# Global attention: VectorE evicts the first transposed group of each unit, GpSimd makes the mask rows of every second head

## The chip, the cores and the metric

The kernel runs on one NeuronCore of a Trainium2 chip. The metric is the device time of one execution in microseconds (us), lower is better. In the text PE is TensorE, DVE is VectorE, ACT is ScalarE, POOL is GpSimd.

## The reference

The input `x` has 2048 rows of 128 values. Three residual stages follow each other: half a feed-forward/local-attention stack of six layers, one global attention, and the same stack again.

```
x = x + 0.5 * ffn_stack(layernorm(x))     # six layers, local attention in windows of 32
x = x + global_attention(layernorm(x))    # the stage that the change touches
x = x + 0.5 * ffn_stack(layernorm(x))
```

The global attention, cut to what matters (L = 2048 rows, 4 heads of 32 values, `x` already normalised):

```
q_in = x @ Wq.T
q, k, v = split(q_in @ Wqkv.T + bqkv)                  # 4 heads each
scores = einsum(q, k) / sqrt(L)
thr[l, h] = sigmoid(relu(q_in) @ Wop.T @ W2.T + b2) * L + WINDOWS[h]
dist[l, m] = m - l   (1e18 where m < l)
s2 = where(dist > thr, -1e18, scores) + scores
out = softmax(s2) @ v
```

Keys in front of the query are masked, so a tile of 128 queries needs only the keys from its own first row on.

## The kernel before

The queries are cut into 16 tiles `t` of 128 rows. Tile `t` needs `m = 16 - t` blocks of 128 keys. A **unit** `n = 2t + pair` is one tile with two of the four heads (`e = 0, 1`), so there are 32 units (`G_UNITS`), and the number of keys falls from 2048 in units 0 and 1 to 128 in units 30 and 31. A unit's keys are cut into **chunks** of up to 512 columns, `c = 0, 1, ...` (four for m = 13 to 16, three for 9 to 12, two for 5 to 8, one for 1 to 4). All four engines run a fixed, hand-written order over the units, and semaphores join them:

- DVE makes the mask rows of a unit ahead of time (`mask_rows`, L743: compare the distance with a threshold per query and multiply by -1e18, SBUF to SBUF, a whole row of keys at once). For each chunk and head it adds mask and scores from PSUM and takes the maximum (`masked_scores`, L756), then reduces the maxima (L764) and signals `g_nmx`. In even units from 4 on, behind chunk 0, it does `update` (L726, L730) for the tile that was attended before: it adds the result to the residual. Some updates also hold layer-norm statistics (L489, L493) or a layer-norm (L502) for the next stage.
- ACT takes the exponential of a whole row for both heads (L974), and evicts the transposed probabilities from PSUM to SBUF, group by group (L964, signal `g_pt_sb`). It does the groups of unit n-1 first and then the exponentials of unit n. It also copies the attended output (L958).
- PE computes scores (L1294), transposes the probabilities in **groups** of up to four 128x128 blocks (`transpose_group`, L1302), multiplies with the values (`attend`, L1313) and transposes the output (L1332). The groups of a unit are those of head e = 0 in order of chunks, then those of e = 1. They use three PSUM banks in turn (`t_bank`: two of ps_t and one of ps_h), so group g waits until group g-3 has been evicted.
- POOL does two small operations for each layer-norm part (`layer_norm_rstd`, L412 and L414), and otherwise waits until the stage is over.

PE's order in iteration n of its loop: the scores of chunks 0 and 1 of unit n; then, for odd n, `attend((n-3)/2)`, or for even n the small output transpose; then the groups of unit n-1 two at a time, with a later chunk of unit n behind each two. An **odd iteration** thus has an attend and an **even iteration** has none.

The rows of the profile name tiles by memory: `arena` is the big SBUF block that holds scores, masks and probabilities; `w_vo` and `w_qk` hold the masks of odd units. The score chunks lie in `ps_a` and `ps_s`.

Of the kernel before, what the change touches and what calls it, by code (L numbers as in the profile page):

```python
# [8 lines left out]
ALU = mybir.AluOpType  # L9
# [3 lines left out]
P = 128  # L13
# [99 lines left out]
def build(nc, x, fWqkv, fqs, fks, fWo, fg, fb, fW1, fb1, fW2, fb2,  # L113
# [5 lines left out]
    with ctx:  # L119
# [125 lines left out]
        def s_bank(k, e):  # L245

            return (A, S)[k % 2][:, e * 512:e * 512 + 512]

        def t_bank(gidx):

            return (T[0], T[1], H[1][:])[gidx % 3]
# [9 lines left out]
        def ln_bank(n, g):  # L261
# [2 lines left out]

        (const_in, gain_in, late_in, id_in, x_in, w0_in, w1_in, w_in, g_win, zero_done, misc_done, cast_done, out_done) = map(
            sem, "const_in gain_in late_in id_in x_in w0_in w1_in w_in g_win zero_done misc_done cast_done out_done".split())
        start_lo, start_hi = map(sem, "start_lo start_hi".split())
        (ln_stats, ln_mv, ln_rstd, ln_norm, ln_ps, ln_lo) = map(
            sem, "ln_stats ln_mv ln_rstd ln_norm ln_ps ln_lo".split())
# [135 lines left out]
        def _(pool):  # L405
            pool.memset(half_pow[:], -0.5).then_inc(misc_done, 1)

            def layer_norm_rstd(part):

                n, t0, t1 = LN_PARTS[part]  # L410
                pool.wait_ge(ln_mv, part + 1)
                pool.tensor_scalar(rstd[:, t0:t1], mv[:, t0:t1, 1], EPS, None, ALU.add).then_inc(ln_rstd, 1)  # L412
                pool.wait_ge(ln_rstd, 2 * part + 1)
                pool.tensor_tensor(rstd[:, t0:t1], rstd[:, t0:t1], half_pow[:, t0:t1], ALU.pow).then_inc(ln_rstd, 1)  # L414
# [57 lines left out]
                make_table(Step(0, 0), u)  # L472
            steps(0, body)
            pool.wait_ge(halo, UNITS)
            for part in range(1, 7):
                layer_norm_rstd(part)
            pool.wait_ge(g_upd, TILES)
            zero_blocks()
            for u in range(2):
# [4 lines left out]
        def _(dve):  # L484
# [252 lines left out]
                    dve.wait_ge(g_upd, t + 1)  # L737
                    layer_norm_stats(3 + t // 4)

            def mask_rows(n, e):  # L740
                t, keys = n // 2, L - n // 2 * P
                h = n % 2 * 2 + e
                dve.tensor_scalar(g_mask[n % 2][e][:, 0:keys], g_dist[:, 0:keys], g_thr[:, t, h:h + 1], -BIG,  # L743
                                  ALU.is_gt, ALU.mult).then_inc(g_msk, 1)

            def masked_scores(n):
                b = n % 2
                last = len(g_chunks[n]) - 1
                dve.wait_ge(g_msk, 2 * n + 2)
                if n >= 2:  # L750
                    dve.wait_ge(g_tps, g_groups[n - 2][-1][0] + 1)
                for k, c, w in g_chunks[n]:
                    for e in range(2):
                        cols = slice(c * 512, c * 512 + w)
                        dve.wait_ge(g_sps, 2 * k + e + 1)
                        dve.tensor_tensor_reduce(g_s[b][e][:, cols], s_bank(k, e)[:, 0:w], g_mask[b][e][:, cols],  # L756
                                                 2.0 / float(L) ** 0.5, -3.0e38, ALU.add, ALU.max,
                                                 g_mx[:, b, e, c:c + 1]).then_inc(g_smx, 1)
                    if n + 1 < G_UNITS and 1 <= c < last:
                        mask_rows(n + 1, c - 1)  # L760
                    if c == 0 and last > 0 and n >= 4 and n % 2 == 0:
                        update((n - 4) // 2)
                dve.wait_ge(g_smx, 2 * g_chunks[n][-1][0] + 2)
                dve.tensor_reduce(g_nm[:, b, :], g_mx[:, b, :, 0:len(g_chunks[n])], AX, ALU.max, negate=True)\  # L764
                   .then_inc(g_nmx, 1)
                if last == 0 and n % 2 == 0:
                    update((n - 4) // 2)
                if n + 1 < G_UNITS:
                    for e in range(max(last - 1, 0), 2):
                        mask_rows(n + 1, e)  # L770

            mask_rows(0, 0)
            mask_rows(0, 1)
            for g in range(4):
                values(g)
            dve.wait_ge(y2_ps, DUOS)
# [1 line left out]
            for n in range(G_UNITS + 4):  # L778
                if n < G_UNITS:
                    masked_scores(n)  # L780
                elif n % 2 == 0:
                    update((n - 4) // 2)
            layer_norm(6)
# [7 lines left out]
        def _(act):  # L791
# [161 lines left out]
            for n in range(G_UNITS + 2):  # L953
                if n >= 3 and n % 2 == 1:
                    t = (n - 3) // 2
                    act.wait_ge(g_ops, t + 1)
                    wait(act, g_ops2, t)
                    act.activation(g_ot, H[0][:, 0:P], ACT.Copy).then_inc(g_otsb, 1)  # L958
                if 1 <= n <= G_UNITS:
                    t, pair = (n - 1) // 2, (n - 1) % 2  # L960
                    wait(act, g_ops, t)
                    for gidx, e, c, w in g_groups[n - 1]:
                        act.wait_ge(g_tps, gidx + 1)
                        act.activation(g_pt[2 * pair + e][:, c * 512:c * 512 + w], t_bank(gidx)[:, 0:w], ACT.Copy)\  # L964
                           .then_inc(g_pt_sb, 1)
                if n < G_UNITS:
                    t = n // 2
                    act.wait_ge(g_nmx, n + 1)
                    if t >= 2:
                        act.wait_ge(g_rsd, t - 1)  # L970
                    for e in range(2):
                        h = n % 2 * 2 + e
                        row = g_s[n % 2][e][:, 0:L - t * P]
                        act.activation(row, row, ACT.Exp, bias=g_nm[:, n % 2, e:e + 1],  # L974
                                       accum_out=g_sum[:, GH * (t % 2) + h:GH * (t % 2) + h + 1]).then_inc(g_exp, 1)
# [6 lines left out]
        def _(pe):  # L982
# [314 lines left out]
            def transpose_group(n, group):  # L1297
                gidx, e, c, w = group
                pe.wait_ge(g_exp, 2 * n + e + 1)
                wait(pe, g_pt_sb, gidx - 2)  # L1300
                for k in range(w // P):
                    last = pe.transpose(t_bank(gidx)[:, k * P:(k + 1) * P],  # L1302
                                        g_s[n % 2][e][:, c * 512 + k * P:c * 512 + (k + 1) * P], ident[:])
                last.then_inc(g_tps, 1)

            def attend(t):
                pe.wait_ge(g_pt_sb, g_groups[2 * t + 1][-1][0] + 1)
                pe.wait_ge(g_zc, 1)
                wait(pe, g_upd, t)
                for k in range(TILES - t):  # L1310
                    for h in range(GH):
                        c = slice(h * GD, (h + 1) * GD)
                        last = pe.matmul(H[0][c, 0:P], g_v[:, t + k, c], g_pt[h][:, k * P:(k + 1) * P],  # L1313
                                         start=(k == 0), stop=(k == TILES - t - 1), skip_group_check=True)
                last.then_inc(g_ops, 1)
# [3 lines left out]
            for n in range(G_UNITS + 4):  # L1319
# [19 lines left out]
                while issued < here:  # L1339
                    scores(*stream_of_chunks[issued])  # L1340
                    issued += 1
            pe.wait_ge(g_pt_sb, g_groups[-1][-1][0] + 1)
            pe.wait_ge(g_smx, 2 * g_chunks[-1][-1][0] + 2)
            for g in range(4):
                ln_transposes(2, g)
# [58 lines left out]
```

## Time and profile before

| what | value |
|---|---|
| median of 3 runs | 3391.22 us (3385.19 to 3392.05) |
| the profiled execution | 3389.85 us |
| its span, first to last instruction | 3388.0 us |
| global attention in it, first scores to last output copy | about 1620.1 to 1824.0 us |
| PE, DVE, ACT, POOL busy, share of the span | 95%, 87%, 75%, 75% |

Times inside the profile are microseconds from the start of the span. A matmul's duration includes its way through the engine, so two that follow each other overlap by some 0.1 to 0.2 us, and starts are the better measure. DVE's and ACT's instructions overlap by about 0.1 us in the same way.

### The profile page before, as it was taken

How to read it: one execution, taken by the hardware profiler on the slowest of the kernel's cores; microseconds unless marked ns; L12 is line 12 of the kernel's file. 1: busy time of each engine (PE TensorE's matmuls, PEld its weight loads, DVE VectorE, ACT ScalarE, POOL GpSimd, SP SyncE). 2: the span in 40 equal slices, each digit the busy share in tenths (PEclk: the TensorE clock that was granted, in tenths of full speed). 3: DMA queues.
4: the chain of work that ended last, by engine and by line, in shares of the span. 5: the costliest groups of instructions: out<-in, count | busy, mean ns of one | idle time of the engine just before them, and what ended most of it. 6: DMA issues, size and time to landing. Idle time of an engine off the chain costs nothing. (4 is left out here: it accounts for less than half of the span.)

```text
span 3388.0 us, 103004 instructions
## 1 busy us (share of the span) xinstructions
PE 3218.7 (95%) x42016; PEld 2199.1 (65%) x42016; DVE 2962.3 (87%) x5370; ACT 2528.7 (75%) x4368; POOL 2538.7 (75%) x1365
## 2 busy tenths in 40 slices
PE   6999999999999999997997899999999999999997
PEld 3666666666666666664564566666666666666665
DVE  7989999899999899994677899899999999999995
ACT  4777777777877777873586777777787778777873
POOL 7888888888888788880003988788888888888881
PEclk9999999999999999998798999999999999999998
DMA  2110010010010000001000000000000000000000
GB/s 82 50 31 2 21 31 2 21 31 2 21 31 2 21 18 2 2 14 37 1 2 33 2 2 2 33 2 2 33 2 2 33 2 2 34 2 2 2 2 14
DMA packets 31050, 53.30 MB, mean 16 GB/s; under 512 B 11510, under 2 KB 24054, under 8 KB 27254
## 3 DMA queue, kind: packets, MB, share of 16 engines
q1 hardware_dynamic: 30582, 46.71, 4.2%
q8 instruction: 337, 5.52, 0.7%
q14 instruction: 131, 1.07, 0.1%
HBM read 37.26 MB, written 9.44 MB: 14 GB/s over the span
## 5 line engine op out<-in xcount | busy, mean ns | idle before, releaser
L447 POOL TENSOR_TENSOR arena<-arena 128x1024 f32<-128x1024 f32 x384 | 722.8, 1903 | 395.7 <-DVE arena L552 395.7
L440 POOL TENSOR_TENSOR arena<-arena 128x1024 f32<-128x1024 f32 x384 | 906.8, 2361 | 30.6 <-DVE arena L562 0.5
L431 POOL TENSOR_TENSOR arena<-arena 128x1024 f32<-128x1024 f32 x384 | 767.1, 1998 | 51.3 <-ACT arena L808 38.1
L1053 PE MATMUL ps_a<-w_qk,stream 128*128 128x512 f32 x1536 | 757.0, 616 | 13.1 <-DVE arena L562 11.7
L1068 PE MATMUL ps_h<-arena,w_vo 128*128 128x256 f32 x3072 | 730.7, 381 | 11.9 <-DVE arena L552 6.1
L808 ACT ACTIVATE arena<-ps_a 128x512 f32<-128x512 f32 x768 | 418.9, 602 | 315.0 <-PE ps_a L1053 305.6
L1068 PEld LDWEIGHTS ps_h<-arena,w_vo 128*128 128x128 f32 x3072 | 562.9, 191 | 86.0 <-issue 7.7
L562 DVE TENSOR_TENSOR arena<-ps_a,arena 128x1024 f32<-128x1024 f32 x384 | 467.1, 1216 | 50.1 <-ACT arena L808 49.5
L568 DVE TENSOR_REDUCE arena<-arena 128x16 f32<-128x1024 f32 x384 | 462.8, 1205 | 36.1 <-ACT arena L814 36.0
L1046 PE MATMUL ps_t<-ident,arena 128*128 128x128 f32 x3072 | 402.0, 274 | 29.8 <-ACT arena L819 21.2
L814 ACT ACTIVATE arena<-arena 128x1024 f32<-128x1024 f32 x384 | 413.4, 1077 | 8.7 <-ACT arena L808 0.4
L1053 PEld LDWEIGHTS ps_a<-w_qk,stream 128*128 128x128 f32 x1536 | 264.3, 192 | 226.7 <-issue 194.7
L1046 PEld LDWEIGHTS ps_t<-ident,arena 128*128 128x128 f32 x3072 | 352.6, 141 | 82.5 <-issue 50.5
L1063 PE MATMUL ps_a<-arena 32*128 32x512 f32 x1536 | 382.9, 616 | 15.4 <-DVE arena L624 13.4
L1063 PE MATMUL ps_t<-arena 32*128 32x512 f32 x1536 | 382.9, 616 | 0.0
L891 ACT ACTIVATE arena<-ps_a 128x1024 f32<-128x1024 f32 x192 | 196.6, 1024 | 225.4 <-PE ps_t L1063 225.4
L1079 PE MATMUL ps_h<-arena,w 128*128 128x256 f32 (+1 forms) x1152 | 309.4, 392 | 9.5 <-ACT arena L846 5.4
L1222 PE MATMUL ps_s<-arena 64*32 64x64 f32 x24576 | 292.9, 226 | 23.2 <-issue 23.2
L1222 PEld LDWEIGHTS ps_s<-arena 64*32 64x32 f32 x24576 | 257.1, 105 | 67.8 <-issue 67.7
L1079 PEld LDWEIGHTS ps_h<-arena,w 128*128 128x128 f32 (+1 forms) x1152 | 198.0, 180 | 125.8 <-issue 85.1
L610 DVE TENSOR_REDUCE arena<-ps_s 128x16 f32<-128x1024 f32 x192 | 234.2, 1220 | 47.4 <-ACT ps_s L841 47.4
L589 DVE TENSOR_REDUCE arena<-ps_s 128x16 f32<-128x1024 f32 x192 | 233.5, 1216 | 27.5 <-PE ps_s L1222 27.2
(163 smaller groups left out, 5011.2 us busy)
## 6 DMA issues: line engine op xcount, KB each, us to landing
w_qk<-fWqkv SPq DMA_DIRECT2D x12, 1024.0 KB, 5.3
vo_scr<-w_vo SPq DMA_DIRECT2D x6, 1024.0 KB, 5.6
w_vo<-vo_scr SPq DMA_DIRECT2D x6, 1024.0 KB, 7.3
arena<-fWqkv SPq DMA_DIRECT2D x6, 512.0 KB, 7.7
arena<-fWo SPq DMA_DIRECT2D x6, 512.0 KB, 8.3
w<-fW SPq DMA_DIRECT2D x12, 192.0 KB, 5.6
w<-fW SPq DMA_DIRECT2D x6, 341.0 KB, 3.2
w_scr<-w SPq DMA_DIRECT2D x6, 341.0 KB, 7.1
```

The costliest lines, as they stand in the source:

```text
L431: pool.tensor_tensor(swapped.rearrange("p (c d) -> p c d", d=DH), raw[n].rearrange("p (c d) -> p c d", d=DH), tab.unsqueeze(1).to_broadcas ...
L440: pool.tensor_tensor(r, r, swapped, ALU.add).then_inc(add_s, 1)
L447: pool.tensor_tensor(r, r, rn[u % 2][:, n * HEADS:(n + 1) * HEADS].unsqueeze(2) .to_broadcast([P, HEADS, DH]), ALU.mult).then_inc(rot_s, 1)
L562: dve.tensor_tensor(rot[n][u % 2].rearrange("p (h d) -> p h d", d=DH), A[:].rearrange("p (h d) -> p h d", d=DH), tab.unsqueeze(1).to_broad ...
L568: dve.tensor_reduce(ss[:, n * HEADS:(n + 1) * HEADS], square[n].rearrange("p (h d) -> p h d", d=DH), AX, ALU.add).then_inc(red_s, 1)
L808: last = act.activation(dst[:, :, h, :], src[:, :, 1 - h, :], ACT.Copy)
L1046: last = pe.transpose(T[n][:, c % 4 * P:(c % 4 + 1) * P], src[:, c * P:(c + 1) * P], ident[:])
L1053: last = pe.matmul(A[:, n * 512:(n + 1) * 512], stream[:, c0:c0 + P], w_qk[:, u // TILES % 2, off:off + 512], start=True, stop=True)
L1063: last = pe.matmul(dst, x_win[v % 3][r, k, :], src[r, k], start=(k == 0), stop=(k == 1))
L1068: last = pe.matmul(H[1][:, 0:W2T], w_vo[:, duo_layer(d) % 2, h, :], g_t[d % 2][:, h].rearrange("p j t -> p (j t)"), start=(h == 0), stop=( ...
L1079: last = pe.matmul(H[0][0:k, e * W2T:(e + 1) * W2T], w_1[:, duo_layer(d) % 2, off:off + k], xn_t, start=True, stop=True)
L1222: last = pe.matmul(S[w * WIN:(w + 1) * WIN, col:col + SLOTS], q_t[r, c * P + w * WIN:c * P + (w + 1) * WIN], k_t[v % 2][r, c, w * WIN:w * ...
```

## The change

Two pieces of work change their engine.

1. The first transposed group of every unit (head 0, chunk 0) is evicted by DVE instead of ACT (`first_group`, signal `g_pt_first`). In units of three or four chunks DVE does that for unit n-1 behind chunk 1 of unit n and behind the mask rows of unit n+1. In units of one or two chunks it does so behind all chunks, the reduction and the mask rows. ACT leaves the first group out. PE waits for both signals: group g waits until g-3 is evicted, by whichever engine does it.
2. The mask rows of head e = 1 are made by POOL, one unit ahead of DVE, released by `g_nmx`. DVE makes those of e = 0 only, and always before `first_group`. POOL's layer-norm parts 3 to 5 are put between its mask rows of units 11, 19 and 27.

In units of one chunk `update` now stands behind the mask rows and `first_group`.

```diff
             pool.wait_ge(halo, UNITS)
-            for part in range(1, 7):
+            for part in range(1, 3):
                 layer_norm_rstd(part)
+
+            def mask_rows(n):
+                t, keys, h = n // 2, L - n // 2 * P, n % 2 * 2 + 1
+                wait(pool, g_nmx, n - 1)
+                pool.tensor_scalar(g_mask[n % 2][1][:, 0:keys], g_dist[:, 0:keys], g_thr[:, t, h:h + 1], -BIG,
+                                   ALU.is_gt, ALU.mult).then_inc(g_msk_odd, 1)
...
+            for n in range(G_UNITS):
+                mask_rows(n)
+                if n in (11, 19, 27):
+                    layer_norm_rstd(3 + n // 8 - 1)
+            layer_norm_rstd(6)
...
+            def first_group(n):
+                t, pair = n // 2, n % 2
+                gidx, e, c, w = g_groups[n][0]
+                wait(dve, g_ops, t)
+                dve.wait_ge(g_tps, gidx + 1)
+                dve.tensor_copy(g_pt[2 * pair][:, 0:w], t_bank(gidx)[:, 0:w]).then_inc(g_pt_first, 1)
...
-                dve.wait_ge(g_msk, 2 * n + 2)
+                dve.wait_ge(g_msk, n + 1)
+                dve.wait_ge(g_msk_odd, n + 1)
...
-                    if n + 1 < G_UNITS and 1 <= c < last:
-                        mask_rows(n + 1, c - 1)
                     if c == 0 and last > 0 and n >= 4 and n % 2 == 0:
                         update((n - 4) // 2)
+                    if c == 1 and last > 1:
+                        mask_rows(n + 1)
+                        if n >= 1:
+                            first_group(n - 1)
...
+                if last <= 1:
+                    if n + 1 < G_UNITS:
+                        mask_rows(n + 1)
+                    first_group(n - 1)
                 if last == 0 and n % 2 == 0:
                     update((n - 4) // 2)
-                if n + 1 < G_UNITS:
-                    for e in range(max(last - 1, 0), 2):
-                        mask_rows(n + 1, e)
...
-                    for gidx, e, c, w in g_groups[n - 1]:
+                    for gidx, e, c, w in g_groups[n - 1][1:]:
                         act.wait_ge(g_tps, gidx + 1)
...
-                wait(pe, g_pt_sb, gidx - 2)
+                wait(pe, g_pt_sb, by_act(gidx - 3))
+                wait(pe, g_pt_first, by_dve(gidx - 3))
...
-                pe.wait_ge(g_pt_sb, g_groups[2 * t + 1][-1][0] + 1)
+                pe.wait_ge(g_pt_sb, by_act(g_groups[2 * t + 1][-1][0]))
+                pe.wait_ge(g_pt_first, 2 * t + 2)
```

`by_dve(g)` counts the first groups up to group g, `by_act(g)` the others.

## Rows read from the trace of the kernel before

**Rows 1.** The page: its first line.

```profile
span 3388.0 us, 103004 instructions
```

**Rows 2.** Busy time by stretches: length, PE, PEld, DVE, ACT, POOL busy (instructions), granted clock, DMA.

```profile
1730.00:1750.00 20.00, 19.93 (x281) 14.43 (x281) 16.07 (x51) 16.50 (x31) 0.00 (x0) 1.00 0.01 2
...
1818.00:1822.00 4.00, 2.59 (x26) 1.33 (x24) 3.83 (x24) 3.83 (x16) 0.00 (x0) 1.00 0.00 0
```

**Rows 3.** Who waited for whom, 1660 to 1825: us in total, times, longest.

```profile
PE ps_t L1302 <- ACT arena L974: 1.2, 3, 0.4
PE ps_t L1302 <- ACT arena L964: 1.1, 3, 0.6
```

**Rows 4.** Groups of instructions by form: count, busy us, mean ns of one, idle before.

```profile
L964 ACT ACTIVATE arena<-ps_t 128x512 f32<-128x512 f32 x71 | 41.4, 601 | 17.1 <-PE ps_t L1302 16.8
...
L743 DVE TENSOR_SCALAR w_qk<-arena 128x512 f32<-128x512 f32 x1 | 0.5, 481 | 0.0
...
L648 DVE COPY stream<-ps_t 64x512 f32<-64x512 f32 x4 | 2.6, 692 | 0.1
```

**Rows 5.** Timeline of DVE, unit 14: start us, us, what, [idle before].

```profile
1751.01 0.69 DVE L756 CUSTOM_DVE_ANT_0 arena<-ps_a,arena 128x512 f32<-128x512 f32 x1 [0.95 <-PE ps_a L1294]
...
1753.09 1.11 DVE L502 TENSOR_SCALAR arena<-x_res,mv,rstd 128x128 f32<-128x128 f32 x4
...
1755.33 0.82 DVE L743 TENSOR_SCALAR w_vo<-arena 128x1152 f32<-128x1152 f32 x1
1756.06 0.28 DVE L756 CUSTOM_DVE_ANT_0 arena<-ps_a,arena 128x128 f32<-128x128 f32 x1
```

**Rows 6.** Timeline of PE, iteration 14.

```profile
1749.71 1.13 PE L1294 MATMUL ps_a<-arena 32*128 32x512 f32 x4
...
1753.36 1.11 PE L1302 MATMUL ps_t<-ident,arena 128*128 128x128 f32 x6
...
1755.47 1.13 PE L1294 MATMUL ps_s<-arena 32*128 32x512 f32 x4 [0.30 <-DVE arena L756]
...
1757.68 2.39 PE L1313 MATMUL ps_h<-arena 128*32 128x128 f32 x80
```

**Rows 7.** Timeline of DVE: the mask rows that follow chunk 1 in units 6, 12 and 18.

```profile
1692.13 1.08 DVE L743 TENSOR_SCALAR w_vo<-arena 128x1664 f32<-128x1664 f32 x1
...
1741.03 0.88 DVE L743 TENSOR_SCALAR w_vo<-arena 128x1280 f32<-128x1280 f32 x1
...
1779.64 0.68 DVE L743 TENSOR_SCALAR w_vo<-arena 128x896 f32<-128x896 f32 x1
```

**Rows 8.** Timeline of PE: the transposes beside them, and the attend behind unit 18.

```profile
1692.20 0.87 PE L1302 MATMUL ps_t<-ident,arena 128*128 128x128 f32 x6
...
1740.40 1.00 PE L1302 MATMUL ps_t<-ident,arena 128*128 128x128 f32 x7
...
1777.46 0.63 PE L1302 MATMUL ps_h<-ident,arena 128*128 128x128 f32 x4
...
1780.43 1.95 PE L1313 MATMUL ps_h<-arena 128*32 128x128 f32 x64
```

**Rows 9.** Timeline of DVE before the first scores: the mask rows of unit 0.

```profile
1613.97 2.48 DVE L743 TENSOR_SCALAR arena<-arena 128x2048 f32<-128x2048 f32 x2
```

**Rows 10.** The page's costliest groups: POOL in the layer stack.

```profile
L440 POOL TENSOR_TENSOR arena<-arena 128x1024 f32<-128x1024 f32 x384 | 906.8, 2361 | 30.6 <-DVE arena L562 0.5
```

**Rows 11.** Timeline of POOL behind the stage.

```profile
1828.07 2.23 POOL L465 MEMSET arena<- 128x2560 f32 x1
```

**Rows 12.** The instructions of line 502: ns min/median/max, first and last start.

```profile
L502 DVE TENSOR_SCALAR arena<-x_res,mv,rstd x48: 314/340/2229, 14.5 to 1831.0; 128x128 f32<-128x128 f32 x48
```

**Rows 13.** Busy time by stretches, in the layer stack after the stage.

```profile
1858.00:1860.00 2.00, 0.90 (x35) 0.49 (x41) 1.24 (x2) 0.96 (x2) 1.92 (x2) 0.77 0.00 0
1860.00:1862.00 2.00, 2.00 (x124) 1.83 (x106) 1.59 (x9) 0.00 (x0) 1.53 (x1) 0.50 0.01 4
1862.00:1864.00 2.00, 2.00 (x4) 0.53 (x3) 1.93 (x4) 0.00 (x0) 1.45 (x1) 0.88 0.03 8
```

More of the change, by code:

```diff
@@ L247, in s_bank, with by_dve, by_act @@
             return (A, S)[k % 2][:, e * 512:e * 512 + 512]
+        g_first = [groups[0][0] for groups in g_groups]
+        def by_dve(gidx):
+            return sum(g <= gidx for g in g_first)
+        def by_act(gidx):
+            return gidx + 1 - by_dve(gidx) if gidx >= 0 else 0
         def t_bank(gidx):
@@ L266, in build @@
             sem, "const_in gain_in late_in id_in x_in w0_in w1_in w_in g_win zero_done misc_done cast_done out_done".split())
+        g_msk_odd, g_pt_first = map(sem, "g_msk_odd g_pt_first".split())
         start_lo, start_hi = map(sem, "start_lo start_hi".split())
@@ L474, in _ @@
             pool.wait_ge(halo, UNITS)
-            for part in range(1, 7):
+            for part in range(1, 3):
                 layer_norm_rstd(part)
+            def mask_rows(n):
[3 more added lines that the diff above has]
+                                   ALU.is_gt, ALU.mult).then_inc(g_msk_odd, 1)
+            pool.wait_ge(g_win, 16 * G_DMAS)
+            pool.wait_ge(g_thr_done, 1)
+            pool.wait_ge(y2_ps, DUOS)
+            pool.wait_ge(fold_out[1], 32 * DEPTH // 2)
+            for n in range(G_UNITS):
[3 more added lines that the diff above has]
+            layer_norm_rstd(6)
             pool.wait_ge(g_upd, TILES)
@@ L738, in update, with mask_rows @@
                     layer_norm_stats(3 + t // 4)
[L740 to L743, printed above, removed]
+            def mask_rows(n):
+                t, keys, h = n // 2, L - n // 2 * P, n % 2 * 2
+                dve.tensor_scalar(g_mask[n % 2][0][:, 0:keys], g_dist[:, 0:keys], g_thr[:, t, h:h + 1], -BIG,
                                   ALU.is_gt, ALU.mult).then_inc(g_msk, 1)
+            def first_group(n):
[4 more added lines that the diff above has]
+                dve.tensor_copy(g_pt[2 * pair][:, 0:w], t_bank(gidx)[:, 0:w]).then_inc(g_pt_first, 1)
             def masked_scores(n):
@@ L765, in masked_scores @@
                    .then_inc(g_nmx, 1)
+                if last <= 1:
+                    if n + 1 < G_UNITS:
+                        mask_rows(n + 1)
+                    first_group(n - 1)
                 if last == 0 and n % 2 == 0:
                     update((n - 4) // 2)
-                if n + 1 < G_UNITS:
-                    for e in range(max(last - 1, 0), 2):
-                        mask_rows(n + 1, e)
-            mask_rows(0, 0)
-            mask_rows(0, 1)
+            mask_rows(0)
             for g in range(4):
@@ L780, in _ @@
                     masked_scores(n)
+                elif n == G_UNITS:
+                    first_group(n - 1)
+                    update((n - 4) // 2)
                 elif n % 2 == 0:
@@ L1341, in _ @@
                     issued += 1
-            pe.wait_ge(g_pt_sb, g_groups[-1][-1][0] + 1)
+            pe.wait_ge(g_pt_sb, by_act(g_groups[-1][-1][0]))
+            pe.wait_ge(g_pt_first, G_UNITS)
             pe.wait_ge(g_smx, 2 * g_chunks[-1][-1][0] + 2)
```

## The prediction

> **What bounds the kernel now.** I began with the page: the profiled execution has a span of 3388.0 us and a time of 3389.85, so 1.85 us lie around the span, and it stands 1.4 us under the median of 3391.22 [rows 1]. The change touches only the global attention, some 204 us of it, so the next view was busy time by stretches. In the middle of the stage PE is busy 19.9 of 20 us at the full clock, DVE and ACT 16 to 16.5, POOL nothing [rows 2]. PE sets the pace there, DVE and ACT have a fifth to spare. In the last units it is the other way: DVE and ACT 3.83 of 4 us, PE 2.59 [rows 2]. The view of waits says what PE waits for: the transposes for ACT's exponential 1.2 us and for ACT's evictions 1.1 us, over the whole stage [rows 3]; another 2.5 us of such waits are spread over smaller entries. So what ACT's lateness costs PE is under 5 us in all. Then I laid the timelines of DVE and PE beside each other, for the even iterations (no attend) and the odd ones. The reader is to see in them at which moment PE reaches the fourth group of a unit (group 3, the one that reuses the bank of group 0), and how far DVE is at that moment.
>
> **The change, part by part.**
>
> *ACT loses 32 evictions.* One of 128x512 takes 601 ns [rows 4], about 0.5 us of pace. Off ACT that is some 14 us, but ACT isn't the bound before the last units, so it buys at most PE's waits above: 0 to 5 us. I count 0 for units 4 to 24, because the new wait below takes their place.
>
> *DVE loses 32 mask rows, and gets 32 copies.* At 512 keys one mask row is 481 ns, and the nearest row for the copy (PSUM to SBUF, 512 columns, on 64 partitions) is 692 ns [rows 4]. For tiles of many keys DVE gains: the mask row of 1152 keys is 0.82 us [rows 5], that of 1664 is 1.08 [rows 7]. Below about 900 keys (0.68 us at 896 [rows 7]) the copy is the dearer one. As DVE is not the bound in the large tiles, this gain hides behind PE.
>
> *The order of the copy is what costs.* DVE is a queue, and `first_group(n-1)` stands behind chunk 0, the update, chunk 1 and a mask row of unit n. PE can't write group 3 of unit n-1 before that copy. Before, ACT did it between its exponentials, before or soon after PE came there. All numbers for unit 14: PE starts chunk 0 at 1749.71, it takes 1.13, and DVE starts on it at 1751.01, so a handover is 0.17 us (I use 0.15) and DVE is never earlier: this distance is fixed by PE [rows 5, 6]. DVE then works without a gap, with the update and a layer-norm part at 1753.09, to the mask row at 1755.33, and the next instruction starts at 1756.06 [rows 5]. There the copy comes in: 0.69 us, end 1756.75, handover, group 3 at 1756.9. Before, PE was at group 3 at 1753.6 (1753.36 plus two blocks; seven blocks in 1.00 us make 0.12 each with the pipeline's end taken off [rows 6, 8]). PE stands still for 3.3 us. Behind it come ten blocks (1.25 us) and two chunks (1.95), so the attend starts at 1760.1 and not at 1757.68. The loss is 2.4 us, as PE had lost some 0.9 there already, partly to DVE (0.30) [rows 6].
>
> The same reading elsewhere, with the mask row's pace 0.08 under its duration:
> - Unit 6 (four chunks, stands for 4, 6, 8): mask row 1692.13, copy 1693.13 to 1693.82, group 3 at 1693.96, before 1692.69 [rows 7, 8]. Loss 1.25 each, 3.7.
> - Units 10, 12, 14, 16 (two groups of three): unit 12 has no layer-norm work: mask row 1741.03, group 3 at 1742.66, before 1740.77 [rows 7, 8], loss 1.9. Units 10 and 16 come out between 12 and 14. Sum 8.8.
> - Units 18, 20, 22 (two chunks; the copy stands behind the reduction too): for 18 the mask row is at 1779.64, the copy ends at 1780.92, group 3 at 1781.1 instead of 1777.46. With its four blocks and the two chunks the attend starts at 1783.3 instead of 1780.43 [rows 7, 8]. Loss 2.9, in 20 and 22 a bit less (no statistics; shorter chunks). Sum 7.8.
> - Unit 24: the same in small, 1.1.
>
> Together 21.4 us. Nothing gives it back: in the odd iterations PE is the bound from its first chunk on, and everything there is placed relative to PE. In them the attend (2 us and more) stands before the transposes, and DVE has the copy done in time, but for units 19 to 23, where I count 0.5 in all. In units 0 to 3 PE runs at half speed and there is no update: 0.
>
> *The last units* (25 to 31, DVE-bound [rows 2]): a copy costs 0.1 to 0.2 us more than the mask row it replaces, `update(14)` now waits for the copy of unit 31 in front of the last attend, ACT saves 0.3 per unit. I take +1.5, bounds -1.5 (ACT's saving counts) and +3.
>
> *POOL's mask rows.* The trace has no such instruction. Bounds for 2048 keys: a memset of 2560 columns took 2.23 us [rows 11], thus 1.8; a two-input operation of 1024 columns took 2361 ns [rows 10], thus 4.7. It has one input, so I take 2.3. It has a whole unit's time (8 us and more at that size, 2 us at 256 keys), so it is hidden at either end. But the two engines block each other: L502 on DVE normally takes 340 ns and once 2229, just as POOL's memset of 2.23 us had begun before it [rows 11, 12]. The mask row is the same kind of instruction (SBUF to SBUF, with a scalar per query). POOL starts on unit n+1 as unit n-1 is reduced, over 4 us before DVE's mask row in the even units to 16, so they seldom meet: 0 there. For unit 0 they meet: DVE's mask row (1.2 us, before 2.48 for two, from 1613.97 [rows 9]) waits for POOL's, which began at about 1613.3. With 2.3 us it ends about when the two did: 0, bounds -1.2 and +2.7.
>
> The Trainium skill (GPSIMD Engine Reference, Key points) says that GpSimd shares its SBUF interfaces with VectorE and contends with instructions in a two-port mode. The trace agrees with its 2229 ns.
>
> *PE's clock.* PE now has gaps of about 3 us (units 10, 14, 16, 18, 22). In the layer stack the granted clock fell to 0.50 after PE had been idle for half of a stretch, and was below full for about 3.4 us (0.23, 1.0 and 0.12 of 2 us each, at half) [rows 13]. Each such stretch costs up to 1.7 us of PE work. I count four, 7 us; bounds 0 and 17 (five, each twice as long).
>
> Sum: 21.4 + 0.5 + 1.5 + 0 + 7 = 30.4. On 3389.85 that makes 3420.3, on the median 3421.6: 3421.
>
> **The rivals.**
> - *PE's gain decides* (ends faster). If `first_group` came before PE needs the bank, PE would lose its waits for ACT, 5 us, and the start 1.2. Time 3385. It decides if DVE gets from chunk 0 to the end of the copy in less than what PE needs for two chunks, the output transpose and three groups, about 4 us. The rows give DVE 5.7 in unit 14, 4.3 of it before the mask row [rows 5]. For it speaks only that DVE is busy 16 of 20 us. Chance 0.05.
> - *The delay is absorbed*: DVE, with shorter mask rows, runs ahead and PE finds slack in the odd iterations, 0 to 6 us lost: 3394. Against it: PE 19.9 of 20 [rows 2]. Chance 0.09.
> - *The stall alone*, the clock stays full: 3414. Chance 0.2.
> - *The engines block each other* in the units of two chunks, where the reduction releases both mask rows at once. If POOL gets in first, DVE's stands behind it, in front of the copy: 1 to 2 us in 5 units, 3429. Against it: DVE's starts about 0.15 us earlier. Chance 0.1.
> - *The clock stays low* over several iterations: PE's remaining work, some 80 us at full speed from unit 10 on, would run at half speed for a third or more: 3447. Chance 0.08. The Trainium skill (TensorE: Matmul & The Clock Gate, Part 1) says that the engine is throttled by default and that activity releases it; by that rule long gaps are dear, which fits rows 13.
>
> **The numbers.** Forecast, stall and some loss of clock, 0.48. Change below 0.2% (7 us) can't be told from none. Faster 0.05, same 0.09, slower 0.86. The range goes from 3403 (the stall alone with the smaller ends of its terms) to 3440; it leaves out the two rivals below and the clock that stays low.
>
> **What the profile after would show.** Right: PE waits at L1302 for DVE's copy (a new line), about ten times, 1 to 4 us each, some 20 us in all, every one in an even iteration. DVE's waits for score chunks in even iterations go, ACT has more idle. The stage is 25 to 30 us longer, POOL has 32 instructions of 2 to 5 us at first. The granted clock dips behind units 14, 18 and 22. Wrong: if the copies end before ACT's evictions of group 1, or if DVE's mask rows are stretched to POOL's length. The forecast fails most easily by a shorter chain on DVE before the copy, and by the clock.

## The result, and the profile after

| | median | lowest to highest | ratio to before |
|---|---|---|---|
| before | 3388.32 us | 3385.19 to 3392.05 | |
| after | 3449.68 us | 3444.65 to 3452.59 | 1.0175 [1.0157, 1.0193] |

The change makes the kernel 1.75% slower, 59 to 61 us. (In brackets, here and below, is the 95% interval of the ratio.) The prediction had the direction and the order of the copy as its cause, but it put the loss at 30.4 us (3421 us on its base of 3391.22), and its range ended at 3440. The profiled execution of after took 3452.59 us. Its page has this first line, and this granted clock in 40 slices:

```profile
span 3450.2 us, 103082 instructions
...
PEclk9999999999999999997887899999999999999998
```

The span is 62.2 us longer than before's [rows 1]. It can be cut into four stretches at marks that both traces have: the end of the thresholds (before 1613.1, after 1617.3), the first score matmul (1620.09, 1631.07), the start of the last output copy (1823.72, 1883.05) and the end. The stretches grew by 4.2, 6.8, 48.4 and 2.9 us. The first arises before any instruction that was touched, nearly all of it in the first 100 us (more of this at the end); for the last no cause is shown. So there are two places to explain, 6.8 us at the start of the stage and 48.4 us in it.

PE's busy time from the first scores to the last output copy, before and then after (stretch, length, busy, instructions, granted clock, DMA):

```profile
1620.09:1823.72 203.63, 194.48 (x1967) 0.92 0.01 3
1631.07:1883.05 251.98, 215.90 (x1967) 0.83 0.02 5
```

The number of matmuls is the same. PE's idle time grew from 9.2 to 36.1 us, that is by 26.9, and the same matmuls took 21.4 us longer. So the 48.4 us have two parts: time in which PE waits, and work at a lower clock. (The second is a net figure: at the beginning of the stage PE is at 0.50 in both kernels, before until about 1658, after until about 1656.)

**In the stage.** The view of waits of after, 1660 to 1885 (who waited for whom: us in total, times, longest):

```profile
DVE arena L790 <- PE ps_a L1333: 40.7, 22, 4.2
...
PE ps_t L1342 <- DVE arena L777: 19.7, 8, 3.3
...
PE ps_h L1342 <- DVE arena L777: 7.2, 5, 3.6
```

L1342 is the transposes, L777 the new copy: 13 waits, 26.9 us. Before, the transposes lost 1.2 and 1.1 us to ACT in the same view [rows 3]. DVE in turn waits 40.7 us for the scores in `ps_a`, before 21.4 (1660 to 1825): the two engines wait for each other by turns. Unit 14 shows how. The timeline of DVE in after:

```profile
1776.81 0.69 DVE L790 CUSTOM_DVE_ANT_0 arena<-ps_a,arena 128x512 f32<-128x512 f32 x1 [1.68 <-PE ps_a L1333]
...
1778.89 1.16 DVE L529 TENSOR_SCALAR arena<-x_res,mv,rstd 128x128 f32<-128x128 f32 x4
...
1781.18 0.81 DVE L769 TENSOR_SCALAR w_vo<-arena 128x1152 f32<-128x1152 f32 x1
1781.92 0.68 DVE L777 COPY arena<-ps_t 128x512 f32<-128x512 f32 x1
```

and the timeline of PE:

```profile
1779.16 0.44 PE L1342 MATMUL ps_t<-ident,arena 128*128 128x128 f32 x2
1782.74 1.09 PE L1342 MATMUL ps_t<-ident,arena 128*128 128x128 f32 x4 [3.14 <-DVE arena L777]
...
1785.04 2.07 PE L1333 MATMUL ps_s<-arena 32*128 32x512 f32 x4
1786.90 1.91 PE L1333 MATMUL ps_a<-arena 32*128 32x512 f32 x4
1788.75 4.36 PE L1354 MATMUL ps_h<-arena 128*32 128x128 f32 x80
```

Up to the gap everything is as in [rows 5, 6], shifted in time: DVE does chunk 0's reduction, the update, the layer norm, chunk 1, the mask row, and only then the copy. PE stands still for 3.14 us. But after it the chunks take 2.07 and 1.91 us in place of 1.13, and the attend 4.36 in place of 2.39 [rows 6]: that is TensorE at the lower of its two levels, 1.2 in place of 2.4 GHz. In stretches of 2 us the granted clock is 1.00 up to 1782, through most of the gap, and 0.50 from 1784 to 1792, though PE is busy all that time. PE in the last of these stretches and the one behind it (length, busy, granted clock, DMA):

```profile
1790.00:1792.00 2.00, 2.00 (x48) 0.50 0.04 8
1792.00:1794.00 2.00, 2.00 (x32) 0.79 0.00 0
```

The same over most of the stage, in stretches of 20 us:

```profile
1670.00:1690.00 20.00, 17.39 (x115) 0.84 0.00 1
1690.00:1710.00 20.00, 18.04 (x202) 0.93 0.00 1
1710.00:1730.00 20.00, 18.59 (x200) 0.93 0.01 2
1730.00:1750.00 20.00, 17.18 (x183) 0.93 0.01 2
1750.00:1770.00 20.00, 18.23 (x179) 0.87 0.00 1
1770.00:1790.00 20.00, 16.86 (x177) 0.81 0.00 1
1790.00:1810.00 20.00, 17.03 (x185) 0.76 0.01 2
1810.00:1830.00 20.00, 16.15 (x151) 0.83 0.00 1
1830.00:1850.00 20.00, 14.11 (x146) 0.94 0.01 2
1850.00:1870.00 20.00, 17.43 (x183) 0.89 0.00 1
```

Before, every such stretch from 1670 to 1810 had 1.00, as the one shown in [rows 2]. Here the missing shares add up to 1.27, or 25 us of full-speed work not done in 200 us. That is an upper bound of what the clock costs there, as PE was idle in a part of the low spells; the busy times above say 21.4 for the whole stage.

**At its start.** POOL, DVE and PE around the first mask rows of after (three timelines):

```profile
1617.45 7.17 POOL L492 TENSOR_SCALAR arena<-arena 128x2048 f32<-128x2048 f32 x1 [18.44 <-DVE arena L745]
1624.72 8.00 POOL L492 TENSOR_SCALAR w_qk<-arena 128x2048 f32<-128x2048 f32 x1
```

```profile
1618.14 7.57 DVE L769 TENSOR_SCALAR arena<-arena 128x2048 f32<-128x2048 f32 x1
1625.62 1.27 DVE L724 TENSOR_TENSOR arena<-ps_a,arena 128x512 f32<-128x512 f32 x2
...
1636.08 1.28 DVE L769 TENSOR_SCALAR w_vo<-arena 128x2048 f32<-128x2048 f32 x1
```

```profile
1626.44 3.75 PE L1302 MATMUL ps_a<-arena 128*128 128x128 f32 x16 [7.30 <-DVE arena L724]
...
1631.07 2.08 PE L1333 MATMUL ps_a<-arena 32*128 32x512 f32 x4 [0.88 <-DVE arena L724]
```

POOL's mask row takes 7.17 us (3.5 ns a column), where the prediction's bounds were 1.8 and 4.7 us. DVE's own row, 1.28 us by itself (third DVE row), takes 7.57 beside it: it ends at 1625.71, 1.1 us behind the end of POOL's, so it had to let POOL's go first. The values and so the scores stand behind it.

The two engines met again in the stage, where the prediction had nothing for it. DVE's mask row of unit 2 took 4.16 us in place of 1.22, that of unit 4 2.99 in place of 1.15, and those of units 3, 5 and 7 took 1.57, 2.26 and 1.60. These rows stand in front of the copies in iterations 1 to 4 and 6.

### The profile page after: what moved, and what is told of

Same layout as the page of the kernel before. It is cut to its first block and busy times, and to the rows that moved or that the text cites. A ratio compares the mean times of both kernels' runs of the same rounds, so it can differ in the third digit from the quotient of the medians.

```text
span 3450.2 us, 103082 instructions
## 1 busy us (share of the span) xinstructions
PE 3244.4 (94%) x42016; PEld 2215.7 (64%) x42016; DVE 2971.2 (86%) x5370; ACT 2518.3 (73%) x4336; POOL 2668.7 (77%) x1397
## 3 DMA queue, kind: packets, MB, share of 16 engines
q14 instruction: 130, 1.06, 0.1%
## 5 line engine op out<-in xcount | busy, mean ns | idle before, releaser
L930 ACT ACTIVATE arena<-ps_a 128x1024 f32<-128x1024 f32 x192 | 196.7, 1024 | 227.8 <-PE ps_t L1102 227.8
```

## The experiments

The runs of before beside them had a median of 3389.02 us (13 runs, beside experiments 1 to 3), 3389.91 (17, beside 4, 5, 6 and 9) and 3390.06 (17, beside 7 and 8). Single runs of before lie between 3376.35 and 3401.55. Each diff is against the changed kernel and shows its main lines.

**1. The two halves of the change.** First, DVE evicts and DVE makes all mask rows, head 1's behind the copy:

```diff
                     if c == 1 and last > 1:
                         mask_rows(n + 1)
                         if n >= 1:
                             first_group(n - 1)
+                    if c == 2 and last > 2:
+                        mask_rows(n + 1, 1)
```

> DVE evicts the first group where the change has it, all mask rows stay on DVE (the rows of head 1 behind the copy, so that the way to the copy is as in the changed kernel). Order theory (the loss comes from where the copy stands in DVE's queue, and from the clock that PE loses in the gaps): some 21 us of gaps and some 20 us of clock, 3425 to 3438. POOL theory (the loss comes from POOL's slow mask rows and what they block on DVE): most of it goes, 3388 to 3402.

Measured: 3439.69 us (3437.80 to 3442.27), ratio 1.0147 [1.0130, 1.0164]. The waits of its transposes for the copy, 1650 to 1870:

```profile
PE ps_t L1342 <- DVE arena L770: 18.8, 9, 3.6
...
PE ps_h L1342 <- DVE arena L770: 6.2, 4, 3.6
```

So 50 of the 60 us are here (1.7 us above the range that was given), with 25.0 us of such waits, and its first scores came at 1620.05, as before. Then the other half, POOL's mask rows with ACT evicting all groups:

```diff
                     if c == 1 and last > 1:
                         mask_rows(n + 1)
-                        if n >= 1:
-                            first_group(n - 1)
...
-                    for gidx, e, c, w in g_groups[n - 1][1:]:
+                    for gidx, e, c, w in g_groups[n - 1]:
```

> POOL makes the mask rows of head 1 as in the changed kernel, ACT evicts every group as before. Order theory: only the 7 us in front of the first scores remain, 3393 to 3400, no gaps at the fourth group. POOL theory: 3420 or more.

Measured: 3392.81 us (3389.04 to 3400.01, 10 runs), ratio 1.0008 [0.9994, 1.0021]. So POOL's work alone does not slow the kernel down. In its trace the late start is there (first scores to last output copy: 1632.4 to 1830.8, PE's wait of 7.3 us for the values as above), but the stage is 198.4 us long, before 203.6.

**2. The copy earlier.** In even iterations it goes right behind chunk 0, in front of the update:

```diff
                     if c == 0 and last > 0 and n >= 4 and n % 2 == 0:
+                        first_group(n - 1)
                         update((n - 4) // 2)
...
-                        if n >= 1:
+                        if n in (1, 2) or n % 2:
                             first_group(n - 1)
```

> The changed kernel, but in even units from 4 on DVE's copy stands right behind chunk 0, in front of the update and chunk 1. Order theory: the gaps and with them the clock's loss go, the start's 7 us stay: 3393 to 3402. POOL theory: no change from the changed kernel, 3440 to 3455.

Measured: 3418.77 us (3415.98 to 3424.20), ratio 1.0090 [1.0069, 1.0111]. 31 us came back, not 50. The waits for the copy were down to 4.2 us. In their place PE waits for the score banks that DVE's reductions free, as its timeline in iteration 14 and its waits (1650 to 1850) show:

```profile
1768.81 1.13 PE L1335 MATMUL ps_s<-arena 32*128 32x512 f32 x4 [1.62 <-DVE arena L790]
```

```profile
PEld ps_s L1335 <- DVE arena L790: 11.4, 14, 2.1
PE ps_s L1335 <- DVE arena L790: 6.2, 8, 1.6
```

In unit 14 chunk 1's reduction now starts 4.14 us behind chunk 0's, before 3.10 (1751.01 to 1754.11): 0.6 us for the copy and 0.4 in which DVE waits for the group to be transposed. Over the stage PE's idle time is 22.0 us (before 9.2, after 36.1) and its busy time 195.6 (before 194.5): with waits of at most 1.62 us the clock cost little. It still dipped: two of the stretches of 20 us from 1670 to 1830 have 0.91, and behind the wait shown the attend took 3.81 us in place of 2.39. The stage is 13.9 us longer than before's. Of the rest of the loss 6.8 us are the start; 4.9 lie in front of the thresholds and behind the stage.

**3. The clock by itself.** Everything as in the changed kernel, but PE makes 14 spare transposes of the identity while it waits for the copy, in every second unit from 9 to 21. They add nothing to the computation.

```diff
+                if n % 2 and 9 <= n <= 21 and group == g_groups[n][3]:
+                    pe.wait_ge(g_upd, (n - 3) // 2 + 1)
+                    for _ in range(14):
+                        pe.transpose(H[0][:, 384:512], ident[:], ident[:])
                 wait(pe, g_pt_sb, by_act(gidx - 3))
```

> The changed kernel with 14 extra transposes of the identity (written to a part of ps_h that nobody reads) in front of the fourth group of units 9 to 21, behind a wait for the update that DVE has done by then; they fit into the gap, so DVE's way is the same. If the lower clock is a cause by itself: the clock stays up in most of units 9 to 22 and 10 to 20 us come back, 3428 to 3440. If the gaps alone are the cause: 3448 to 3455, as the filling adds nothing but a little PE work.

Measured: 3430.51 us (3427.46 to 3433.02), ratio 1.0119 [1.0102, 1.0136]: 19.2 us less than the changed kernel, with more work on PE and the copy as late as ever. Its stretches, all engines (PE, PEld, DVE, ACT, POOL, clock, DMA), where after has 0.87, 0.81 and 0.76:

```profile
1750.00:1770.00 20.00, 19.84 (x282) 14.50 (x281) 14.55 (x46) 13.44 (x25) 11.20 (x3) 1.00 0.01 2
1770.00:1790.00 20.00, 18.44 (x187) 12.79 (x187) 13.82 (x53) 14.07 (x29) 11.57 (x3) 1.00 0.00 1
1790.00:1810.00 20.00, 16.93 (x182) 11.88 (x186) 13.21 (x46) 11.62 (x23) 11.82 (x6) 1.00 0.01 2
```

The stage is 232.9 us long, 19.1 less than the changed kernel's. The clock is a cause of its own, and nearly three times the 7 us of the prediction.

**4. The start by itself.** DVE makes both mask rows of unit 0, POOL begins behind them with unit 1:

```diff
-            for n in range(G_UNITS):
+            for n in range(1, G_UNITS):
                 mask_rows(n)
...
             mask_rows(0)
+            mask_rows(0, 1)
```

> The changed kernel, but both mask rows of unit 0 are made by VectorE, and GpSimd begins with unit 1, once VectorE's two are done. In the changed kernel GpSimd's first mask row took 7.17 us and VectorE's, beside it, 7.57 us in place of 1.28, and the stage's first score matmul ran 13.8 us behind the thresholds, before 7.0. Theory A (that block costs the time at which the stage starts, one for one): first scores 7 to 9 us behind the thresholds, and 5 to 7 us off the whole, 3443 us (3440 to 3446). Rival (the start is made up later, since every unit is bound by something else): the same time as the changed kernel within 2 us, 3448 to 3452.

Measured: 3440.37 us (3437.53 to 3450.08), ratio 1.0151 [1.0130, 1.0172]. 9.3 us less by the medians, though the two intervals overlap. Where the start is concerned the trace is plain, with POOL, DVE and PE in turn:

```profile
1622.00 7.18 POOL L494 TENSOR_SCALAR w_qk<-arena 128x2048 f32<-128x2048 f32 x1 [21.50 <-DVE arena L771]
```

```profile
1619.32 2.47 DVE L771 TENSOR_SCALAR arena<-arena 128x2048 f32<-128x2048 f32 x2
...
1624.17 0.69 DVE L726 TENSOR_TENSOR arena<-ps_a,arena 128x512 f32<-128x512 f32 x1 [1.18 <-PE ps_a L1305]
```

```profile
1626.72 1.13 PE L1336 MATMUL ps_a<-arena 32*128 32x512 f32 x4 [0.88 <-DVE arena L726]
```

The thresholds ended at 1618.5, so the first scores came 8.2 us behind them, in the changed kernel 13.8: 5.5 us are back at the start. What that brings at the end this trace can't show: the profiled execution took 3450.08 us, the slowest of its four, and its stage was 257.4 us long, 5.4 more than the changed kernel's. So the gain rests on the medians, here and in experiment 8. DVE's additions at L726 keep their 0.69 us while POOL is in the middle of its mask row: not every pair of instructions blocks. This kernel and the first of experiment 1 differ almost only in who makes head 1's mask rows behind unit 0, and take 3440.4 and 3439.7 us. So POOL's rows cost no more in the stage than the same rows on DVE, as far as medians tell. The traces show a small price: in iterations 1, 2, 4 and 6 of after PE waits 1.20, 1.10, 2.12 and 1.57 us for the copy, in the first kernel of experiment 1 not at all, 0.88, 1.01 and 1.06. That is 3.0 us more.

**5. How the loss goes with the length of the gap.** The copy in front of the mask row, both still behind chunk 1:

```diff
                     if c == 1 and last > 1:
-                        mask_rows(n + 1)
                         if n >= 1:
                             first_group(n - 1)
+                        mask_rows(n + 1)
```

> The changed kernel, but VectorE copies the first transposed group in front of the mask row instead of behind it (both still behind chunk 1). TensorE's wait for the copy gets shorter by one mask row (1.0 us at 1280 keys, 0.3 at 256) in each even unit from 4 on. Theory A (each us of gap costs a us, the clock's loss stays as it is): 6 to 8 us less, 3442 us. Theory B (the clock's loss goes with the length of the gaps): the granted clock of 1750 to 1810 rises above the changed kernel's 0.81 and 0.76, and 12 to 20 us less, 3430 to 3438. Rival (VectorE's queue sets the units and its order does not matter): within 2 us of the changed kernel.

Measured: 3424.80 us (3409.04 to 3432.14), ratio 1.0097 [1.0066, 1.0128]. Its waits, 1650 to 1860, and two of its stretches:

```profile
PE ps_t L1342 <- DVE arena L777: 12.8, 7, 2.8
...
PE ps_h L1342 <- DVE arena L777: 4.3, 4, 3.0
```

```profile
1770.00:1790.00 20.00, 17.67 (x199) 12.51 (x201) 11.17 (x36) 9.20 (x20) 8.97 (x4) 0.76 0.01 2
1790.00:1810.00 20.00, 16.73 (x162) 11.13 (x155) 12.24 (x40) 11.54 (x22) 8.84 (x5) 0.88 0.00 1
```

The waits are 9.8 us shorter, the time 24.9 us: 2.5 us for each us of gap, more than either theory had. In the trace the stage is 25.5 us shorter than the changed kernel's, 9.7 of it idle time and 15.9 busy time. That speaks for theory B's kind of loss and against a fixed price of the clock, though not in the stretches that I had named: they have 0.76 and 0.88, and the clock came back in those from 1670 to 1750, all at 1.00 (after 0.84 to 0.93). There the waits for the copy in iterations 4 to 10, 2.12, 1.57, 1.14 and 2.66 us long in after, were gone but for 0.17 and 1.80 us. The four runs lie 23 us apart, far for so few; no trace shows why.

**6. The update out of the way too.** The early copy, unit 0 on DVE, and the update behind the reduction in even iterations:

```diff
                     if c == 0 and last > 0 and n >= 4 and n % 2 == 0:
-                        update((n - 4) // 2)
+                        first_group(n - 1)
...
+                if last > 0 and n >= 4 and n % 2 == 0:
+                    update((n - 4) // 2)
```

> VectorE copies right behind chunk 0 in even units, as in the early copy, the update of the output rows goes behind the reduction in even units, and unit 0's mask rows are both VectorE's. Theory A (in the early copy what was left was chunk 1's reduction standing behind update and copy, with TensorE waiting 1.1 to 1.6 us for a score bank per even unit): the waits of the scores for the masked scores' banks go, and with the start 6 us earlier the time is 3385 to 3400. Rival (the copy on VectorE itself is too much in even units, wherever it stands): 3405 to 3415, the early copy's 3419 less the start alone.

Measured: 3418.60 us (3407.96 to 3423.39), ratio 1.0078 [1.0060, 1.0096]. The median is above both ranges. The waits for score banks went indeed (6.1 us, 24.8 in the early copy and 9.4 before; these sums count PE and PEld each, whose waits overlap), and still nothing was gained, not even what the start brings. The waits for copies are back, 11.7 us of them where the early copy has 4.2:

```profile
PE ps_t L1348 <- DVE arena L779: 8.8, 6, 3.5
...
PE ps_h L1348 <- DVE arena L779: 2.9, 4, 1.2
```

The longest of them come in odd iterations, into which the late update pushes DVE's work. For 3.5 us of it, in iteration 11, the cause is the other half of the change. DVE and PE there:

```profile
1737.39 4.51 DVE L771 TENSOR_SCALAR arena<-arena 128x1280 f32<-128x1280 f32 x1
1741.82 0.67 DVE L779 COPY arena<-ps_t 128x512 f32<-128x512 f32 x1
```

```profile
1742.64 1.08 PE L1348 MATMUL ps_t<-ident,arena 128*128 128x128 f32 x4 [3.53 <-DVE arena L779]
```

DVE's mask row of 1280 keys takes 4.51 us in place of 0.88, because POOL's, held up by a layer-norm part, had begun 0.8 us earlier (1736.61 to 1741.23). Behind the gap PE's clock falls (0.78 from 1730 to 1750). So this kernel can't settle whether the copy fits on DVE in the even iterations; the same order with all mask rows on DVE wasn't run. The waits of 1.94 and 1.80 us in iterations 19 and 23, where the mask row in front of the copy keeps its time (0.61 and 0.48 us), show that a part of the delay is DVE's own.

**7. Is it the even iterations alone?** DVE copies in odd iterations only; in even ones ACT evicts as before. Unit 0 on DVE.

```diff
-        g_first = [groups[0][0] for groups in g_groups]
+        g_first = [groups[0][0] for groups in g_groups[::2]]
...
                         mask_rows(n + 1)
-                        if n >= 1:
+                        if n % 2:
                             first_group(n - 1)
```

> The changed kernel with unit 0's mask rows by VectorE, and VectorE copies the first transposed group in odd iterations only, where it makes no update; in even ones ScalarE evicts it as before. Theory A (only the even iterations, where update, chunk 1 and mask row stand ahead of the copy, make TensorE wait): 3386 to 3393, no different from before, with no TensorE wait for VectorE's copy over 0.5 us. Rival (a copy in any iteration delays VectorE's reductions): half of the changed kernel's loss stays, 3405 to 3415.

Measured: 3392.51 us (3384.32 to 3402.27, 12 runs), ratio 1.0011 [0.9998, 1.0024]. The only waits for the copy, 1650 to 1830:

```profile
PE ps_h L1343 <- DVE arena L779: 0.6, 2, 0.3
```

The half of the copies that stands in odd iterations costs nothing that can be measured, with POOL making its mask rows as in the changed kernel (but unit 0's). The loss in the stage comes with the other half.

**8. Do the parts add up?** Experiments 3 and 4 at once, the spare transposes in units 3 to 21:

```diff
+                if n % 2 and 3 <= n <= 21 and group == g_groups[n][3]:
+                    pe.wait_ge(g_upd, (n - 3) // 2 + 1)
+                    for _ in range(14):
+                        pe.transpose(H[0][:, 384:512], ident[:], ident[:])
```

> The changed kernel with both repairs of size at once: unit 0's mask rows by VectorE (alone: 9.3 us less) and the 14 spare transposes in front of the fourth group in the even iterations, now from iteration 4 on (units 3 to 21; alone for units 9 to 21: 19.2 us less). VectorE still copies behind chunk 1 and the mask row. The spare transposes stand for work that keeps the clock up, and are no part of the computation. Theory A (the loss is a sum of three: start, clock, and TensorE's idle time itself): 3417 to 3424, that is 28 to 35 us above before, the size of the waits for the copy (28 us), with the granted clock of 1670 to 1850 at 0.95 or more. Rival (start and clock overlap, the late start being partly a clock loss): 3426 to 3432.

Measured: 3421.82 us (3418.62 to 3427.84), ratio 1.0102 [1.0079, 1.0125], 27.9 us less than the changed kernel; 9.3 and 19.2 make 28.5. One of its stretches, and PE in an odd iteration:

```profile
1790.00:1810.00 20.00, 17.47 (x202) 12.57 (x205) 14.03 (x56) 12.09 (x24) 10.32 (x5) 1.00 0.00 1
```

```profile
1769.56 2.39 PE L1361 MATMUL ps_h<-arena 128*32 128x128 f32 x80
```

The attend is back at 2.39 us. 31.8 us over before are left. In the trace, 28.1 us longer than before's, the stage has 23.6 of them: PE's idle time is 12.3 us above before's, and its busy time, with the 140 spare transposes, 11.3. The start has 1.3, and 4.1 lie in front of the thresholds, where nothing was touched.

**9. A version faster than both?** POOL's mask rows without its two faults: ACT evicts everything, unit 0 on DVE.

```diff
-            for n in range(G_UNITS):
+            for n in range(1, G_UNITS):
                 mask_rows(n)
...
-                    for gidx, e, c, w in g_groups[n - 1][1:]:
+                    for gidx, e, c, w in g_groups[n - 1]:
```

> GpSimd makes the mask rows of every second head but unit 0's, and ScalarE evicts all transposed groups as before. With GpSimd from unit 0 on, the time was that of the kernel before (ratio 1.0008), its stage 5 us shorter and its start some 6 to 7 us later. Theory A (both are real and add): the start comes back and 4 to 6 us of the stage stay: 3383 to 3387, ratio 0.9982 to 0.9995. Rival (the shorter stage was only the late start being made up): no change, 3388 to 3393.

Measured: 3390.38 us (3381.78 to 3396.22, 12 runs), ratio 0.9998 [0.9985, 1.0010]: no change, as the rival had it. In its trace the stage took 197.0 us (1628.1 to 1825.1), 6.6 less than before, yet the median shows none of it. I can't settle where it went; the start below is a candidate. No kernel here beats the one before by what can be measured.

## Why the prediction was wrong

- **The order of the copy** was the main cause, as forecast, in the iterations and nearly with the sizes forecast; only the waits of 1.20 and 1.10 us in iterations 1 and 2 were not in it. Unit 14: gap 3.3 us expected, 3.14 measured. Waits for the copy: "about ten times, 1 to 4 us each, some 20 us" expected; 13 times, 26.9 us measured. The terms for it (21.4, 0.5 and 1.5) made 23.4; PE's idle time in the stage grew by 26.9. With the clock held up and the start mended (experiment 8), the stage was 23.6 us longer than before's. The term was at most some 3 us too small, about the 3.0 us that POOL's blocks added to the gaps of iterations 1 to 6.
- **The clock** was the step that failed most: "I count four, 7 us; bounds 0 and 17". The spare transposes brought 19.2 us back, over the upper bound, and this in units 9 to 21 alone; the busy times of the whole stage say 21.4. Both factors of the term were too small. I had taken the length of a dip, 3.4 us, from the layer stack [rows 13]: behind the gap of unit 14 PE stayed at half for some 10 us, until the attend was nearly over, at 0.50 from 1784 to 1792. And dips came behind the gaps of units 4 to 8 as well, of which I had counted none (0.84 in the first stretch of 20 us above, where the gap of iteration 4 is 2.12 us). The Trainium skill (TensorE: Matmul & The Clock Gate, Part 1) has the throttled clock as the default that activity lifts. The trace agrees in direction: the clock fell in a gap of 3.14 us and came back after some 10 us of work. The rival built on it, "the clock stays low", 3447 with a chance of 0.08, was the nearest to 3450, in part by luck: it had nothing for the late start and for the 7 us in front of the thresholds and behind the stage.
- **The start** was the second: "0, bounds -1.2 and +2.7", measured +6.8 in the trace of after; experiment 4 brought the first scores 5.5 us nearer to the thresholds, and the median down by 9.3. The block between the two engines was foreseen, and that they meet at unit 0 too. What was wrong is POOL's price: 2.3 us assumed, 7.17 measured. I had argued from one input against two; the row of a two-input operation, 2361 ns for 1024 columns [rows 10], would have given 4.7 for 2048, and even that was too low. A sign that the prediction had named for its own failure, DVE's mask row stretched to POOL's length, is what came (7.57 beside 7.17).
- **POOL hidden in the stage:** right by the time, in spite of that price. Its longest row behind unit 1 was 6.73 us in a unit of some 11, and the kernels of experiments 1 and 4 differ by 0.7 us. But "they seldom meet: 0 there" was wrong: five of DVE's rows were stretched, in units 2 to 5 and 7 and not in the units of two chunks that the rival named, and in experiment 6 such a block made a gap of 3.5 us.
- **Nothing gives it back:** not contradicted. ACT lost 32 evictions and DVE 32 mask rows, and no experiment showed a gain from either that a median could tell.
- **The rivals.** That PE's gain decides "if `first_group` came before PE needs the bank" was tried in experiment 2. The condition was nearly met (4.2 us of such waits were left), and the time was 3418.8, not 3385: in unit 14 the copy and the wait for its group put chunk 1's reduction 1.0 us back, and PE waited for that. It is a wait which neither the forecast nor a rival had. DVE, busy 16 of 20 us on the mean [rows 2], had no room there for the copy in front of chunk 1.

The sum with measured terms, all from the trace of after: idle time in the stage 26.9 (forecast 23.4), work at the lower clock 21.4 (7), start 6.8 (0), in front of the thresholds 4.2 and behind the stage 2.9 (no term; no cause shown), together 62.2. Experiment 8 adds that start and clock are separate: mended together they bring 27.9 us (with spare transposes in three units more), mended one by one 28.5. It says nothing of the other terms.

## What to carry to other kernels

A mean busy share of 80% hides that work comes in alternating iterations: before a job is put on a helping engine, lay out that engine's queue in the fullest iteration, and ask which of its results the bounding engine wants first. Gaps on TensorE, here of 1.1 to 3.6 us, can cost more than their length: count the idle time, and then expect nearly the same again for the work behind it at half clock (here 21 us on top of 27). With fewer and shorter ones (experiment 2, none over 1.62 us) the same matmuls took only 1 us longer than before. Price an engine on the very instruction it will run, and if no row shows it, don't let a simpler instruction set the lower end. If two engines block each other, an experiment that moves work in time can make them meet anew: look for stretched instructions before you read its result.

## What the runs showed of the hardware

- GpSimd's compare and multiply with a scalar per partition runs at some 3.5 ns a column of float32 (7.17 us at 2048, 3.70 at 1024, 0.72 at 128); VectorE does it in 1.28 us at 2048 when nothing is beside it. The Trainium skill (GPSIMD Engine Reference, 4.1 Engine selection) calls one-input work on GpSimd roughly line-rate; the measurement decides here, and it is 5.6 times VectorE's time.
- The same instruction on VectorE, SBUF to SBUF, stood still while GpSimd's ran and ended 1.1 us behind it (7.57 us for 1.28), and one that began in the middle of another was stretched to 4.16 us at 1920 keys. It goes the other way too: GpSimd's second row, which began 1.0 us before VectorE's ended, took 8.00 us, in experiment 4 7.18. Reductions and additions that read PSUM kept their 0.69 us beside it. The Trainium skill (SBUF — State Buffer, SBUF: two separate sides) describes the shared port pair as an exclusive lock for a whole instruction, and the trace agrees.
- Spare transposes of the identity, some 0.12 us each, in a gap that is there anyway kept TensorE at 2.4 GHz (experiment 3: 1.00 in every stretch of 20 us from 1730 to 1830, where after has 0.76 to 0.93) and made a kernel with more instructions 19 us faster.
- The profiled executions of after and of the ten experiments reached the same instruction near 1517 us at -0.3 to +8.1 us beside before's. In after, 5.0 us were there at 80 us already, and stayed within a microsecond or so; in experiment 7 and the early copy most of the delay came later (0.2 and 0.5 at 80 us). The kernels with GpSimd's mask rows came between 1.5 (the early copy) and 8.1 us late (the spare transposes of experiment 3), the one without them at -0.3. With one profile for each kernel, and runs of before that differ by 25 us, this doesn't tell chance from effect; if it isn't chance, it would explain why the shorter stage of experiment 9, 5.7 us late in its trace, gave no gain.
